# Perceiver on one core: the second layer's self attention with weights divided ahead of their turn, and scores and values in another matmul form

## The chip, the cores and the metric

The kernel runs on one core of a Trainium2 chip. The time is the device time of one execution in microseconds (us). TensorE multiplies matrices into PSUM, VectorE and ScalarE work element by element and read PSUM, GpSimd works on SBUF; they run at the same time and wait for each other by semaphores. A matmul has a stationary operand, loaded first, and a moving one that streams through. All work in the changed stage is fp32.

## The reference

x has 128 batches of 32 tokens with 128 features, the context 128 batches of 257 rows. Four layers follow each other, each a cross attention, a self attention and a feed-forward part, twelve stages in all, each added to x after a layer norm. The stage that is changed is the second layer's self attention (8 heads of 32, keys and values through a latent of 64):

```python
q = (x @ Wq.T).reshape(b, t, N_HEADS, HEAD_DIM)
kv_latent = x @ Wkv_down.T
k = (kv_latent @ Wk_up.T).reshape(b, t, N_HEADS, HEAD_DIM)
v = (kv_latent @ Wv_up.T).reshape(b, t, N_HEADS, HEAD_DIM)
scores = jnp.einsum('bqhd,bkhd->bhqk', q, k) * scale
attn = jax.nn.softmax(scores, axis=-1)
out = jnp.einsum('bhqk,bkhd->bqhd', attn, v)
out = out.reshape(b, t, N_HEADS * HEAD_DIM)
return out @ Wo.T
...
x = x + _L1_attn_ref(_layernorm(x, axis=-1), L1_attn_Wq, L1_attn_Wkv_down, L1_attn_Wk_up, L1_attn_Wv_up, L1_attn_Wo)
```

## The kernel before

x stays in SBUF as 32 tiles of 128 tokens, four batches of 32 each (NB = 4). The twelve stages run one after the other; at the end of each all five engines drain and wait for each other. `self_attention` writes the self attentions of the last three layers; `kind` tells them apart, and the changed stage is `"L1"` (layers are numbered from 0). Each engine has a function `one(r)` that issues its part of round r, and `Plan.run` calls it for the rounds from -3 to 32, the middle ones as a hardware loop of two rounds. The order in a round is the order of the lines, the same for all rounds. Rounds overlap: in round r the tile r + 3 gets its statistics, r + 2 is normalised, turned and projected, r + 1 gets its keys, values and scores, r its softmax, and r - 1 has its weights applied and is put out.

For one tile, the queries (256 features: 8 heads of 32) come as two halves n = 0, 1 of four heads, features on partitions. `rows_by_head` spreads each half into `qbd`: for each batch b a block of 128 columns, one for each pair of head j and query, that is zero outside the head's 32 features. In `scores` (L1039) such a block is the stationary operand, and the keys of its own batch, 32 columns, are the moving one. So the scores of one head and query lie on one partition, with 8 groups (half and batch) of 32 keys along it.

VectorE takes the maximum of each group (L1285) and subtracts it (L1287), ScalarE takes the exponential in place (L1209), and TensorE turns the undivided weights, 128 columns at a time (`turn`, L1062); ScalarE copies them to SBUF (L1132). Meanwhile VectorE sums the weights (L1300), takes reciprocals (L1301), and multiplies these with a mask of heads into `w` (L1302).

GpSimd writes `vm` (L933): the values of a tile once for each batch, zero outside that batch's rows. `values` (L1072) has the turned weights of a half as the stationary operand and 512 columns of `vm`, four batches by 128 features, as the moving one. The rows of the result are pairs of head and query; in each only the features of its own head are wanted. VectorE multiplies by `w`, which divides and clears the rest (L1268), and `heads` (L1084) sums the rows over the heads with eight matmuls by a window of a 0/1 matrix. The result is features by tokens; ScalarE copies it (L1167), `output` multiplies by Wo (L1092), and VectorE adds it to x (L1277).

On TensorE a round reads, in this order: `middle` (keys and values of the next tile from the latent, L1014, L1016), `values`, `turn_x` (L990), `turn` (L1062), `project` (L996, L998), `heads`, `scores`, `output`.

Of the kernel before, what the change touches and what calls it, by code (L numbers as in the profile page):

```python
# [881 lines left out]
def self_attention(k, kind, s):  # L882
# [9 lines left out]

    def chain_steps(has):
        if kind == "L1":
            return (["max"] * has.own + ["stats"] * has.third + ["rs", "rr", "w"] * has.own)
        if kind == "L2":
            return (["cos", "sin", "low", "high"] * has.coming + ["stats"] * has.third + ["rr", "w"] * has.turned
                    + ["ms"] * has.after)
        return (["E"] * has.own + ["rr", "w"] * has.turned + ["R", "max"] * has.own + ["stats"] * has.third)
# [9 lines left out]
    turned_written, turned_read, pv_done, heads_ready, heads_written, heads_read, out_written, out_read = (  # L909
        PerTile(k.sig(n), 1) for n in ("probs_T_written", "probs_T_read", "pv_done", "heads_ready", "heads_written",  # L910
                                       "heads_read", "out_written", "out_read"))
# [74 lines left out]
    def pe(pe):  # L986
# [44 lines left out]
        def scores(t):  # L1031
            pe.wait_ge(operands.sem, operands.at(t, 1))
            pe.wait_ge(scores_read.sem, scores_read.at(t + -1, 1))
            if kind == "L1":
                pe.wait_ge(mid_read.sem, mid_read.at(t, 1))
                for n in range(2):
                    for b in range(NB):
                        at = n * P + 32 * b
                        mm = pe.matmul(D[:, at:at + 32], s["qbd"][:, n, b * P:(b + 1) * P], s["kv"][:, at:at + 32],  # L1039
                                       start=True, stop=True, skip_group_check=True)  # L1040
            else:
                pe.wait_ge(spread.sem, spread.at(t, 1))
# [13 lines left out]
            mm.then_inc(scores_written.sem, 1)  # L1056
# [8 lines left out]
        def values(t):  # L1065
            pe.wait_ge(turned_read.sem, turned_read.at(t, 1))
            pe.wait_ge(vm_ready.sem, vm_ready.at(t, 1))
            pe.wait_ge(heads_ready.sem, heads_ready.at(t + -1, 1))
            for n in range(nt):
                left, vm = s["pT"][:, n * P:(n + 1) * P], s["vm"][:, t.odd, :]  # L1070
                if kind == "L1":
                    mm = pe.matmul(O[n][:, :], left, vm[:, n * 512:(n + 1) * 512], start=True, stop=True)  # L1072
                else:
                    pe.matmul(batches_first(O[0])[:, :, n, :], left, batches_first(vm)[:, :, n, :], start=True, stop=True,
                              skip_group_check=True)
                    mm = pe.matmul(SUM[:, 4 * n:4 * n + 4], left, k.c("quad"), start=True, stop=True, skip_group_check=True)
            mm.then_inc(pv_done.sem, 1)

        def heads(t):
            pe.wait_ge(heads_ready.sem, heads_ready.at(t, 1))  # L1080
            pe.wait_ge(out_read.sem, out_read.at(t + -1, 1))
            for n in range(2 if kind == "L1" else 1):
                for b in range(NB):
                    mm = pe.matmul(OUT[:, n * P:(n + 1) * P], s["om"][:, n, b * P:(b + 1) * P], window(k, b),  # L1084
                                   start=(b == 0 and n == 0), stop=(b == NB - 1), skip_group_check=True)
            mm.then_inc(heads_written.sem, 1)

        def output(t):
            pe.wait_ge(heads_read.sem, heads_read.at(t, 1))
            if kind == "L1":  # L1090
                for n in range(2):
                    mm = pe.matmul(OUT[:, 256:384], s["outT"][:, n, :], wo[:, n, :], start=(n == 0), stop=(n == 1),  # L1092
                                   skip_group_check=True)
            else:
                mm = pe.matmul(OUT[:, 256:384], s["outT"][:, 0, :], wo[:, :], start=True, stop=True, skip_group_check=True)
            mm.then_inc(out_written.sem, 1)

        def one(r):
# [3 lines left out]
                values(r.t + -1)  # L1102
            if r.after:
                turn_x(r.t + 2)
            if kind == "L1" and r.own:
                turn(r.t)
            if r.after:
                project(r.t + 2)
            if kind == "L2" and r.coming:
                middle(r.t + 1)  # L1110
            if kind == "L3" and r.coming:
                scores(r.t + 1)
            if r.turned:
                heads(r.t + -1)
            if kind == "L2" and r.own:
                turn(r.t)
            if kind != "L3" and r.coming:
                scores(r.t + 1)
            if kind == "L3" and r.own:
                turn(r.t)  # L1120
            if r.turned:
                output(r.t + -1)
# [5 lines left out]
    def act(act):  # L1128
# [33 lines left out]
                act.activation(s["qkT"], MID[:, 0:2 * P], ACT.Copy).then_inc(mid_read.sem, 1)  # L1162

        def take_heads(t):
            n = 2 if kind == "L1" else 1
            act.wait_ge(heads_written.sem, heads_written.at(t, 1))
            act.activation(s["outT"][:, 0:n, :], OUT[:, 0:n * P].rearrange("p (t c) -> p t c", t=n), ACT.Copy  # L1167
                           ).then_inc(heads_read.sem, 1)

        def one(r):  # L1170
            if kind != "L3" and r.turned:
# [32 lines left out]
            if kind == "L1":  # L1204
                if r.coming:
                    take_middle(r.t + 1)
                if r.own:
                    act.wait_ge(scores_read.sem, scores_read.at(r.t, 1))
                    act.activation(s["pr"][:, 0:256], s["pr"][:, 0:256], ACT.Exp).then_inc(probs_ready.sem, 1)  # L1209
# [19 lines left out]
    def dve(dve):  # L1229
# [27 lines left out]
        def heads(r):  # L1257
            if not r.turned:
                return
            t = r.t + -1  # L1260
            if kind != "L1":
                over_sums(r)
            dve.wait_ge(pv_done.sem, pv_done.at(t, 1))
            dve.wait_ge(heads_written.sem, heads_written.at(t + -1, 1))
            w = s["w"].rearrange("p u j -> p (u j)")
            for n in range(2 if kind == "L1" else 1):
                m = 16 if kind == "L1" else 64
                ins = dve.tensor_tensor(s["om"][:, n, :].rearrange("p (g d) -> p g d", d=hd),  # L1268
                                        O[n].rearrange("p (g d) -> p g d", d=hd), bc(w[:, n * m:(n + 1) * m], 2, hd), ALU.mult)
            ins.then_inc(heads_ready.sem, 1)  # L1270

        def residual(r):
            if r.ended if kind == "L2" else r.turned:
# [3 lines left out]
                dve.tensor_tensor(x, x, OUT[:, 256:384], ALU.add).then_inc(out_read.sem, 1)  # L1277

        def one_l1(r):
            sc, pr = D[:, 0:256].rearrange("p (u k) -> p u k", k=32), s["pr"][:, 0:256]  # L1280
            nm, w = s["nm"][:, 0:8], s["w"][:, 0:8, :]
            normalised(r)
            if r.own:
                dve.wait_ge(scores_written.sem, scores_written.at(r.t, 1))
                link(dve.tensor_reduce(nm, sc, X_AXIS, ALU.max, negate=True), r, "max")  # L1285
                dve.wait_ge(turned_written.sem, turned_written.at(r.t + -1, 1))
                dve.tensor_tensor(pr.rearrange("p (u k) -> p u k", k=32), sc, bc(nm, 2, 32), ALU.add  # L1287
                                  ).then_inc(scores_read.sem, 1)
            heads(r)
            if r.coming:  # L1290
                t = r.t + 1
                dve.wait_ge(qkv_read.sem, qkv_read.at(t, 1))
# [3 lines left out]
                ins.then_inc(operands.sem, 1)  # L1296
            stats(r)
            if r.own:
                dve.wait_ge(probs_ready.sem, probs_ready.at(r.t, 1))
                link(dve.tensor_reduce(s["rs"][:, 0:8], pr.rearrange("p (u k) -> p u k", k=32), X_AXIS, ALU.add), r, "rs")  # L1300
                link(dve.reciprocal(s["rr"][:, 0:8], s["rs"][:, 0:8]), r, "rr")  # L1301
                link(dve.tensor_tensor(w, bc(s["rr"][:, 0:8], 2, 4), bc(k.c("quad"), 1, 8), ALU.mult), r, "w")  # L1302
            residual(r)

        def rotate(r):
# [2542 lines left out]
```

## Time and profile before

| | |
|---|---|
| median of 3 runs | 5292.81 us (5286.52 to 6909.59) |
| profiled execution | 5294.46 us |
| its span | 5292.7 us |
| TensorE busy | 4721.4 us, 89% |
| VectorE busy | 3207.9 us, 61% |
| ScalarE busy | 2119.9 us, 40% |
| GpSimd busy | 1841.9 us, 35% |

The 6909.59 us are one execution of the three; the other two are 0.1% apart. The profile is of one execution. PE is TensorE's matmuls, PEld its weight loads, DVE VectorE, ACT ScalarE, POOL GpSimd. An fp32 matmul stands in the trace as two records, so counts of TensorE's rows are twice the matmuls in the code. PEclk is the clock that TensorE was granted, 1.00 being 2.4 GHz and 0.50 1.2 GHz. "Idle before" is the time that an engine sat idle before an instruction, with what released it.

### The profile page before, as it was taken

The numbers are of one execution on the slowest core, as the hardware profiler recorded it, in microseconds if no ns is written. First come the engines' busy times: TensorE is split into PE (matmuls) and PEld (weight loads), VectorE is DVE, ScalarE is ACT, GpSimd is POOL, SyncE is SP. The second block draws the span as 40 slices with busy tenths as digits, with TensorE's granted clock in tenths as the row PEclk, the third lists the DMA queues.
The fourth block names the chain that finished last, engine by engine and source line by source line (L and its number), as shares of the span: only waits on it lengthen the run. The fifth ranks groups of instructions, "written<-read, shape, count | busy, mean of one in ns | idle before, by whom it ended". The sixth has DMA issues, their size and how long they took to land.

```text
span 5292.7 us, 138451 instructions
## 1 busy us (share of the span) xinstructions
PE 4721.4 (89%) x48761; PEld 3730.1 (70%) x48761; DVE 3207.9 (61%) x9513; ACT 2119.9 (40%) x5243; POOL 1841.9 (35%) x2796
## 2 busy tenths in 40 slices
PE   4999999999999999896929999777999989997999
PEld 3777777779867777674627777665577768885776
DVE  4777777756546666565425666685466657764443
ACT  1444444422224444221214555342255545542333
POOL 2555555511113333334143433890034434430000
PEclk8999999999989999896968999898899998888999
DMA  6000000000000000000220100002211100005665
GB/s 201 18 18 18 18 18 18 18 1 2 1 21 29 32 28 25 0 0 20 70 63 29 36 32 28 1 0 55 58 33 32 32 21 0 0 0 114 144 143 134
DMA packets 112436, 199.69 MB, mean 38 GB/s; under 512 B 13315, under 2 KB 54659, under 8 KB 111259
## 3 DMA queue, kind: packets, MB, share of 16 engines
q1 hardware_dynamic: 108147, 188.67, 13.4%
q0 software_dynamic: 4096, 8.40, 0.6%
q8 instruction: 127, 2.08, 0.2%
q14 instruction: 66, 0.54, 0.0%
HBM read 183.29 MB, written 18.97 MB: 38 GB/s over the span
## 4 chain that ended last, share of the span: by engine, by line
PE 75%; DVE 7%; issue 6%; ACT 5%; POOL 4%; SPq 1%; DMA 1%; POOLq 1%; DVEq 0%; ACTq 0%
PE psum_banks L555 6%; PE psum_banks L3075 6%; PE psum_banks L3084 5%; PE psum_banks L560 5%; PE psum_banks L620 4%; PE psum_banks L664 4%; PE psum_banks L671 3%; PE psum_banks L1623 3%; PE psum_banks L624 3%; PE psum_banks L1658 2%; PE psum_banks L2103 2%; PE psum_banks L1084 2%; PE psum_banks L2770 2%; PE psum_banks L1599 2%; ACT scratch L1741 1%
## 5 line engine op out<-in xcount | busy, mean ns | idle before, releaser
L787 DVE TENSOR_REDUCE scratch<-psum_banks 128x2 f32<-128x514 f32 x768 | 531.6, 692 | 411.8 <-PE psum_banks L555 407.8
L706 ACT ACTIVATE scratch<-psum_banks 128x512 f32<-128x512 f32 x768 | 459.4, 598 | 490.0 <-PE psum_banks L565 474.4
L560 PE MATMUL psum_banks<-scratch 32*128 32x128 f32 x6144 | 639.6, 310 | 8.2 <-ACT scratch L706 6.1
L555 PE MATMUL psum_banks<-scratch 32*128 32x257 f32 x3072 | 575.2, 441 | 50.3 <-DVE scratch L788 50.0
L560 PEld LDWEIGHTS psum_banks<-scratch 32*128 32x128 f32 x6144 | 476.6, 185 | 17.5 <-ACT scratch L706 8.6
L555 PEld LDWEIGHTS psum_banks<-scratch 32*128 32x128 f32 x3072 | 253.9, 189 | 272.7 <-issue 175.9
L3084 PEld LDWEIGHTS psum_banks<-w_L_ffn_down,scratch 128*128 128x128 f32 (+1 forms) x2560 | 335.8, 193 | 156.0 <-issue 127.1
L3075 PE MATMUL psum_banks<-scratch,w_L_ffn_up 128*128 128x512 f32 (+1 forms) x752 | 382.0, 603 | 8.2 <-DVE scratch L3262 8.2
L3262 DVE TENSOR_TENSOR scratch<-scratch 128x512 f32<-128x512 f32 x304 | 210.3, 692 | 268.5 <-ACT scratch L3128 234.3
L3128 ACT ACTIVATE scratch<-psum_banks 128x512 f32<-128x512 f32 x320 | 191.0, 598 | 430.1 <-PE psum_banks L3075 430.0
L565 PE MATMUL psum_banks<-shift_T,own_batch 32*128 32x128 bf16 x3072 | 351.2, 215 | 0.0
L3084 PE MATMUL psum_banks<-w_L_ffn_down,scratch 128*128 128x128 f32 (+1 forms) x2560 | 342.7, 277 | 9.0 <-DVE scratch L3262 9.0
L620 PE MATMUL psum_banks<-scratch 128*32 128x128 f32 x6144 | 318.4, 279 | 1.5 <-ACT scratch L706 1.5
L624 PE MATMUL psum_banks<-scratch,consts 128*32 128x128 f32 x6144 | 309.2, 273 | 0.0
L1741 ACT ACTIVATE scratch<-psum_banks,scratch 128x258 f32<-128x258 f32 x512 | 238.6, 473 | 98.4 <-DVE scratch L1826 97.6
L728 ACT ACTIVATE scratch<-psum_banks,c_L_xattn_bk 128x256 f32<-128x256 f32 x384 | 182.8, 476 | 221.4 <-PE psum_banks L671 221.1
L1520 POOL TENSOR_TENSOR scratch<-scratch 128x512 f32<-128x512 f32 x256 | 269.3, 1052 | 0.0
L1599 PE MATMUL psum_banks<-scratch 128*128 128x257 f32 x1024 | 266.9, 383 | 1.3 <-ACT scratch L1758 0.8
L513 POOL TENSOR_TENSOR ln_vareps<-ln_meanvar,ln_eps 128x1 f32<-128x1 f32 x96 | 18.4, 191 | 716.1 <-DVE ln_meanvar L797 716.1
L1623 PE MATMUL psum_banks<-scratch 128*128 128x512 f32 x512 | 247.1, 604 | 11.4 <-ACT scratch L1751 10.6
L1599 PEld LDWEIGHTS psum_banks<-scratch 128*128 128x128 f32 x1024 | 179.7, 190 | 55.4 <-issue 39.8
L933 POOL TENSOR_TENSOR scratch<-scratch,consts 128x512 f32<-128x512 f32 x128 | 134.8, 1064 | 229.1 <-PE psum_banks L1072 139.6
(495 smaller groups left out, 12386.3 us busy)
## 6 DMA issues: line engine op xcount, KB each, us to landing
scratch<-route_T SPq DMA_DIRECT2D x136, 512.0 KB, 7.3
scratch<-in_ctx SPq DMA_DIRECT2D x99, 514.0 KB, 3.5
scratch<-in_ctx_rows SPq DMA_DIRECT2D x130, 128.0 KB, 2.0
scratch<-route_T SPq DMA_DIRECT2D x8, 1024.0 KB, 8.8
expert_rows<-in_ctx SPq DMA_DIRECT2D x10, 512.0 KB, 17.9
scratch<-expert_rows SPq DMA_DIRECT2D x16, 192.0 KB, 2.7
expert_out<-scratch SPq DMA_DIRECT2D x16, 192.0 KB, 2.1
w_L_ffn_up<-in_L_ffn_up SPq DMA_DIRECT2D x1, 2992.0 KB
```

The lines of the kernel that those rows point to most:

```text
L555: return pe.matmul(S[:, g % 2, :], qbd[q, t.odd, (s // 2) * P:(s // 2 + 1) * P], kT_of[q, t.odd, s // 2, :], start=True, stop=True)
L560: return pe.matmul(W[:, g % 2, c * P:(c + 1) * P], kT_of[q, t.odd, b, c * P:(c + 1) * P], qbd[q, t.odd, b * P:(b + 1) * P], start=True, st ...
L565: return pe.matmul(W[:, g % 2, c * P:(c + 1) * P], own_batch[q, b:b + 1].to_broadcast([32, P]), shiftT[q, t.odd, :], start=False, stop=Tru ...
L620: pe.matmul(PV[q, cols], vS[:, t.odd, b, c, q], pT[:, b % 2, g, c, :], start=False, stop=(c == 1), skip_group_check=True)
L624: mm = pe.matmul(SUM[q, cols], k.c("ones")[:, 0:32], pT[:, b % 2, g, c, :], start=False, stop=(c == 1), skip_group_check=True)
L706: act.activation(pT[:, b % 2, 2 * h:2 * h + 2].rearrange("p t c q -> p t (c q)"), W, ACT.Exp).then_inc(exp_ready.sem, 1)
L787: dve.tensor_reduce(parts[:, r.t.odd, 2 * h:2 * h + 2, 0, b], S, X_AXIS, ALU.max, negate=True)
L1599: mm = pe.matmul(S[:, t, 0:KEYS], qa[:, t, b * P:(b + 1) * P], a["zT"][:, b % 2, :], start=True, stop=True, skip_group_check=True)
L1623: mm = pe.matmul(PV[:, :], zk_of[:, b, c, :], a["pT"][:, c, :], start=(c == 0), stop=(c == 1))
L1741: ins = act.activation(a["p"][:, 4 * (b % 2) + t, :], S[:, t, 0:W], ACT.Exp, bias=a["negm"][:, u:u + 1], accum_out=a["rs"][:, u:u + 1])
L3075: mm = pe.matmul(U(u, o)[0:rows(c), :], up_cols(c, o), x, start=True, stop=True)
L3084: mm = pe.matmul(Y[g % 2][:, i * P:(i + 1) * P], a["h"][0:rows(c), u % 3, i * P:(i + 1) * P], down[0:rows(c), c, :], start=(c == 0 and i = ...
```

## The change

All of it is in the stage `"L1"` of `self_attention`:

- VectorE divides the weights by their sums itself (one product of 128x256), and the turn waits for that; the semaphore that ScalarE's exponential gives is now `exp_ready`, and `probs_ready` comes from VectorE. The small product into `w` and the two 128x512 products out of PSUM are gone.
- A block of queries is scored on the keys of all four batches: 128 moving columns for 32, into two PSUM banks instead of one. VectorE reads only the 32 keys of the block's own batch, in two instructions (one a bank) for the maximum and two for the subtraction.
- The values are now the stationary operand, in strips of 32 features (one head), and the turned weights, of all four heads of a group, are the moving one: 32 matmuls of 32x128 for 2 of 128x512. Each strip j writes partitions 32j to 32j + 31, so that the result has features on partitions.
- The sums over heads are gone; ScalarE copies, in four instructions of 32 partitions, for each head the columns that are its own.
- On TensorE the turn of the weights stands behind the scores.

```diff
-            return (["max"] * has.own + ["stats"] * has.third + ["rs", "rr", "w"] * has.own)
+            return (["max"] * has.own + ["stats"] * has.third + ["rs", "rr"] * has.own)
...
                 for n in range(2):
                     for b in range(NB):
-                        at = n * P + 32 * b
-                        mm = pe.matmul(D[:, at:at + 32], s["qbd"][:, n, b * P:(b + 1) * P], s["kv"][:, at:at + 32],
-                                       start=True, stop=True, skip_group_check=True)
+                        mm = pe.matmul(k.bank[n][:, b * P:(b + 1) * P], s["qbd"][:, n, b * P:(b + 1) * P],
+                                       s["kv"][:, n * P:(n + 1) * P], start=True, stop=True, skip_group_check=True)
...
-            pe.wait_ge(heads_ready.sem, heads_ready.at(t + -1, 1))
+            if kind == "L1":
+                pe.wait_ge(heads_read.sem, heads_read.at(t + -1, 1))
+            else:
+                pe.wait_ge(heads_ready.sem, heads_ready.at(t + -1, 1))
...
-                    mm = pe.matmul(O[n][:, :], left, vm[:, n * 512:(n + 1) * 512], start=True, stop=True)
+                    for b in range(NB):
+                        for j in range(4):
+                            d = slice(32 * j, 32 * j + 32)
+                            mm = pe.matmul(O[n][d, b * P:(b + 1) * P], vm[:, n * 512 + b * P + 32 * j:n * 512 + b * P + 32 * j + 32],
+                                           left, start=True, stop=True, skip_group_check=True)
...
-            if kind == "L1" and r.own:
-                turn(r.t)
             if r.after:
                 project(r.t + 2)
...
-            if r.turned:
+            if kind != "L1" and r.turned:
                 heads(r.t + -1)
...
-            if kind == "L3" and r.own:
+            if kind != "L2" and r.own:
                 turn(r.t)
...
+            if kind == "L1":
+                act.wait_ge(pv_done.sem, pv_done.at(t, 1))
+                act.wait_ge(out_written.sem, out_written.at(t + -1, 1))
+                for j in range(4):
+                    d = slice(32 * j, 32 * j + 32)
+                    ins = act.activation(s["outT"][d].rearrange("p n (b q) -> p n b q", q=32),
+                                         k.psum[d, 3:5, :].rearrange("p n (b c) -> p n b c", c=P)[:, :, :, d], ACT.Copy)
+                ins.then_inc(heads_read.sem, 1)
...
-                link(dve.tensor_reduce(nm, sc, X_AXIS, ALU.max, negate=True), r, "max")
+                for n in range(2):
+                    ins = dve.tensor_reduce(nm[:, 4 * n:4 * n + 4], own[n], X_AXIS, ALU.max, negate=True)
+                link(ins, r, "max")
...
-            heads(r)
...
-                link(dve.tensor_tensor(w, bc(s["rr"][:, 0:8], 2, 4), bc(k.c("quad"), 1, 8), ALU.mult), r, "w")
+                dve.tensor_tensor(by_head, by_head, bc(s["rr"][:, 0:8], 2, 32), ALU.mult).then_inc(probs_ready.sem, 1)
```

TensorE's instructions in the second round of the loop, before (the names in brackets are the semaphores waited for):

```order
L1072 MATMUL psum_banks<-scratch 128x512 [waits heads_ready,vm_ready,probs_T_read]
L1072 MATMUL psum_banks<-scratch 128x512
L988 REGISTER_ALU
L990 MATMUL psum_banks<-consts,x_normed 128x128 [waits qkv_read,xn_ready]
L1059 REGISTER_ALU
L1062 MATMUL psum_banks<-consts,scratch 128x128 [waits probs_T_read,probs_ready]
L1062 MATMUL psum_banks<-consts,scratch 128x128
L993 REGISTER_ALU
L996 MATMUL psum_banks<-x_normed_T,w_L_attn_Wq 128x128 [waits xT_read]
...
L1084 MATMUL psum_banks<-consts,scratch 128x128 x7
L1039 MATMUL psum_banks<-scratch 128x32 [waits mid_read,scores_read,operands_ready]
L1039 MATMUL psum_banks<-scratch 128x32 x7
L1092 MATMUL psum_banks<-w_L_attn_Wo,scratch 128x128 [waits heads_read]
```

and now (L1080 values, L993 turn of x, L999 and L1001 projections, L1041 scores, L1064 turn of the weights, L1101 output):

```order
L1080 MATMUL psum_banks<-scratch 32x128 [waits heads_read,vm_ready,probs_T_read]
L1080 MATMUL psum_banks<-scratch 32x128 x31
L991 REGISTER_ALU
L993 MATMUL psum_banks<-consts,x_normed 128x128 [waits qkv_read,xn_ready]
L996 REGISTER_ALU
L999 MATMUL psum_banks<-x_normed_T,w_L_attn_Wq 128x128 [waits xT_read]
...
L1041 MATMUL psum_banks<-scratch 128x128 [waits mid_read,scores_read,operands_ready]
L1041 MATMUL psum_banks<-scratch 128x128 x7
L1061 REGISTER_ALU
L1064 MATMUL psum_banks<-consts,scratch 128x128 [waits probs_T_read,probs_ready]
L1064 MATMUL psum_banks<-consts,scratch 128x128
L1101 MATMUL psum_banks<-w_L_attn_Wo,scratch 128x128 [waits out_read,heads_read]
```

The turn of the weights has moved from between the turn of x and the projections to behind the scores, the sums over heads are gone, and the values are 32 matmuls.

VectorE in a round, now, from the scores' arrival to the divided weights (L1296 maximum, L1300 subtraction, L931 spread queries, L1314 to L1316 sum, reciprocal, division):

```order
L1296 TENSOR_REDUCE scratch<-psum_banks 128x4 [waits scores_written]
L1296 TENSOR_REDUCE scratch<-psum_banks 128x4
L1246 REGISTER_ALU
L1300 TENSOR_TENSOR scratch<-psum_banks,scratch 128x128 [waits probs_T_written,vector_step]
L1300 TENSOR_TENSOR scratch<-psum_banks,scratch 128x128
L1305 REGISTER_ALU
L931 TENSOR_TENSOR scratch<-scratch,consts 128x512 [waits scores_written,qkv_read]
L931 TENSOR_TENSOR scratch<-scratch,consts 128x512
...
L1314 TENSOR_REDUCE scratch<-scratch 128x8 [waits exp_ready]
L1246 REGISTER_ALU
L1315 RECIPROCAL scratch<-scratch 128x8 [waits vector_step]
L1246 REGISTER_ALU
L1316 TENSOR_TENSOR scratch<-scratch 128x256 [waits vector_step]
```

Before, the two products with `w` stood between the subtraction and the spread queries; nothing stands there now.

## Rows read from the trace of the kernel before

**Rows 1.** The page: busy time, share of the span and instructions of each engine.
```profile
PE 4721.4 (89%) x48761; PEld 3730.1 (70%) x48761; DVE 3207.9 (61%) x9513; ACT 2119.9 (40%) x5243; POOL 1841.9 (35%) x2796
```

**Rows 2.** The stage: its us, PE, PEld, DVE, ACT, POOL busy, PEclk, DMA share, GB/s.
```profile
2126.50:2432.70 306.20, 292.63 (x1760) 221.23 (x1760) 180.28 (x448) 74.14 (x224) 88.93 (x128) 0.94 0.00 0
```

**Rows 3.** The chain of waits through one tile: start us, us, what.
```profile
2249.91 0.53 PE psum_banks L1092 x4
2250.44 0.64 PE psum_banks L1014 x4
2251.08 0.43 PE psum_banks L1016 x2
2251.51 1.91 PE psum_banks L1072 x4
2253.43 0.12 PE psum_banks L990
...
2253.57 0.29 ACT x_normed_T L1136
...
2253.90 0.71 PE psum_banks L996 x4
2254.61 0.36 PE psum_banks L998 x2
2254.98 1.98 PE psum_banks L1084 x16
2256.96 1.77 PE psum_banks L1039 x16
```

**Rows 4.** The timeline of the same tile: start us, us, engine, instruction, [idle before].
```profile
2250.60 0.29 DVE L1277 TENSOR_TENSOR x_tokens<-x_tokens,psum_banks 128x128 f32 x1 [1.49 <-PE psum_banks L1092]
...
2251.07 0.42 DVE L1285 TENSOR_REDUCE scratch<-psum_banks 128x8 f32<-128x256 f32 x1
...
2251.68 0.60 ACT L1160 ACTIVATE scratch<-psum_banks 128x512 f32<-128x512 f32 x1 [2.63 <-PE psum_banks L1016]
...
2253.26 0.27 PE L990 MATMUL psum_banks<-consts,x_normed 128*128 128x128 f32 x1
...
2253.37 0.38 PE L1062 MATMUL psum_banks<-consts,scratch 128*128 128x128 f32 x2
2253.46 1.29 DVE L1268 TENSOR_TENSOR scratch<-psum_banks,scratch 128x512 f32<-128x512 f32 x2 [1.52 <-PE psum_banks L1072]
...
2254.67 2.03 DVE L928 TENSOR_TENSOR scratch<-scratch,consts 128x512 f32<-128x512 f32 x2
...
2256.78 0.39 ACT L1143 ACTIVATE scratch<-psum_banks 128x256 f32<-128x256 f32 x1 [2.93 <-DVE scratch L928]
...
2257.06 0.26 ACT L1144 ACTIVATE scratch<-psum_banks 64x128 f32<-64x128 f32 x1
```

**Rows 5.** The chain in the cross attention: matmuls by column groups, 8 records a row.
```profile
1749.85 0.40 PE psum_banks L620 x8
1750.25 0.22 PE psum_banks L624 x8
```

**Rows 6.** TensorE's timeline, first and last outputs; the chain in a slow value stretch.
```profile
2159.94 0.47 PE L1092 MATMUL psum_banks<-w_L_attn_Wo,scratch 128*128 128x128 f32 x2
...
2410.06 0.69 PE L1092 MATMUL psum_banks<-w_L_attn_Wo,scratch 128*128 128x128 f32 x4
...
2431.58 0.60 PE L1092 MATMUL psum_banks<-w_L_attn_Wo,scratch 128*128 128x128 f32 x3 [0.47 <-ACT scratch L1167]
...
2205.76 3.61 PE psum_banks L1072 x4
```

**Rows 7.** TensorE early in the changed stage: us, PE busy, PEclk, DMA.
```profile
2145.00:2150.00 5.00, 5.00 (x22) 0.50 0.01 3
```

**Rows 8.** The fourth layer's self attention (as rows 2), the cross attention (as rows 7).
```profile
4360.00:4760.00 400.00, 369.57 (x2431) 336.96 (x2430) 283.73 (x562) 201.98 (x380) 156.11 (x186) 0.84 0.00 0
...
1745.00:1750.00 5.00, 3.83 (x76) 1.00 0.00 0
```

More of the change, by code:

```diff
@@ L908, in self_attention @@
     spread = PerTile(k.sig("operands_spread"), 1) if kind != "L1" else None
-    turned_written, turned_read, pv_done, heads_ready, heads_written, heads_read, out_written, out_read = (
-        PerTile(k.sig(n), 1) for n in ("probs_T_written", "probs_T_read", "pv_done", "heads_ready", "heads_written",
-                                       "heads_read", "out_written", "out_read"))
+    turned_written, turned_read, pv_done, heads_read, out_written, out_read = (
+        PerTile(k.sig(n), 1) for n in ("probs_T_written", "probs_T_read", "pv_done", "heads_read", "out_written", "out_read"))
+    if kind == "L1":
+        exp_ready = PerTile(k.sig("exp_ready"), 1)
+    else:
+        heads_ready, heads_written = PerTile(k.sig("heads_ready"), 1), PerTile(k.sig("heads_written"), 1)
     if kind == "L1":
@@ L1067, in values @@
             pe.wait_ge(vm_ready.sem, vm_ready.at(t, 1))
-            pe.wait_ge(heads_ready.sem, heads_ready.at(t + -1, 1))
+            if kind == "L1":
+                pe.wait_ge(heads_read.sem, heads_read.at(t + -1, 1))
+            else:
+                pe.wait_ge(heads_ready.sem, heads_ready.at(t + -1, 1))
             for n in range(nt):
@@ L1081, in heads @@
             pe.wait_ge(out_read.sem, out_read.at(t + -1, 1))
[L1082 to L1085, printed above, removed]
+            for b in range(NB):
+                mm = pe.matmul(OUT[:, 0:P], s["om"][:, 0, b * P:(b + 1) * P], window(k, b), start=(b == 0), stop=(b == NB - 1),
+                               skip_group_check=True)
             mm.then_inc(heads_written.sem, 1)
@@ L1090, in output @@
             if kind == "L1":
+                pe.wait_ge(out_read.sem, out_read.at(t + -1, 1))
                 for n in range(2):
@@ L1164, in take_heads @@
         def take_heads(t):
[L1165 to L1168, printed above, removed]
+            if kind == "L1":
+                act.wait_ge(pv_done.sem, pv_done.at(t, 1))
[5 more added lines that the diff above has]
+                ins.then_inc(heads_read.sem, 1)
+            else:
+                act.wait_ge(heads_written.sem, heads_written.at(t, 1))
+                act.activation(s["outT"][:, 0, :], OUT[:, 0:P], ACT.Copy).then_inc(heads_read.sem, 1)
         def one(r):
@@ L1208, in one @@
                     act.wait_ge(scores_read.sem, scores_read.at(r.t, 1))
-                    act.activation(s["pr"][:, 0:256], s["pr"][:, 0:256], ACT.Exp).then_inc(probs_ready.sem, 1)
+                    act.activation(s["pr"][:, 0:256], s["pr"][:, 0:256], ACT.Exp).then_inc(exp_ready.sem, 1)
             if kind == "L2" and r.own:
@@ L1260, in heads @@
             t = r.t + -1
-            if kind != "L1":
-                over_sums(r)
-            dve.wait_ge(pv_done.sem, pv_done.at(t, 1))
+            over_sums(r)
             dve.wait_ge(heads_written.sem, heads_written.at(t + -1, 1))
             w = s["w"].rearrange("p u j -> p (u j)")
[L1266 to L1270, printed above, removed]
+            dve.tensor_tensor(s["om"][:, 0, :].rearrange("p (g d) -> p g d", d=hd), O[0].rearrange("p (g d) -> p g d", d=hd),
+                              bc(w, 2, hd), ALU.mult).then_inc(heads_ready.sem, 1)
         def residual(r):
@@ L1279, in one_l1 @@
         def one_l1(r):
-            sc, pr = D[:, 0:256].rearrange("p (u k) -> p u k", k=32), s["pr"][:, 0:256]
-            nm, w = s["nm"][:, 0:8], s["w"][:, 0:8, :]
+            own = [k.bank[n].rearrange("p (m c) -> p m c", c=32)[:, 0:16:5, :] for n in range(2)]
+            pr = s["pr"][:, 0:256]
+            nm = s["nm"][:, 0:8]
             normalised(r)
@@ L1284, in one_l1 @@
                 dve.wait_ge(scores_written.sem, scores_written.at(r.t, 1))
-                link(dve.tensor_reduce(nm, sc, X_AXIS, ALU.max, negate=True), r, "max")
+                for n in range(2):
+                    ins = dve.tensor_reduce(nm[:, 4 * n:4 * n + 4], own[n], X_AXIS, ALU.max, negate=True)
+                link(ins, r, "max")
                 dve.wait_ge(turned_written.sem, turned_written.at(r.t + -1, 1))
-                dve.tensor_tensor(pr.rearrange("p (u k) -> p u k", k=32), sc, bc(nm, 2, 32), ALU.add
-                                  ).then_inc(scores_read.sem, 1)
-            heads(r)
+                for n in range(2):
+                    ins = dve.tensor_tensor(pr[:, n * P:(n + 1) * P].rearrange("p (u k) -> p u k", k=32), own[n],
+                                            bc(nm[:, 4 * n:4 * n + 4], 2, 32), ALU.add)
+                ins.then_inc(scores_read.sem, 1)
             if r.coming:
@@ L1298, in one_l1 @@
             if r.own:
-                dve.wait_ge(probs_ready.sem, probs_ready.at(r.t, 1))
-                link(dve.tensor_reduce(s["rs"][:, 0:8], pr.rearrange("p (u k) -> p u k", k=32), X_AXIS, ALU.add), r, "rs")
+                dve.wait_ge(exp_ready.sem, exp_ready.at(r.t, 1))
+                by_head = pr.rearrange("p (u k) -> p u k", k=32)
+                link(dve.tensor_reduce(s["rs"][:, 0:8], by_head, X_AXIS, ALU.add), r, "rs")
                 link(dve.reciprocal(s["rr"][:, 0:8], s["rs"][:, 0:8]), r, "rr")
-                link(dve.tensor_tensor(w, bc(s["rr"][:, 0:8], 2, 4), bc(k.c("quad"), 1, 8), ALU.mult), r, "w")
+                dve.tensor_tensor(by_head, by_head, bc(s["rr"][:, 0:8], 2, 32), ALU.mult).then_inc(probs_ready.sem, 1)
             residual(r)
```

## The prediction

> **What bounds the kernel now.** I read the page first: TensorE is busy for 89% of the span, the next engine, VectorE, for 61%, so what TensorE does in the changed stage is the first thing to look at [rows 1]. Twelve stages follow each other with a barrier between them, and only the fifth, the second layer's self attention, is touched; it lasts from 2126.5 to 2432.7 us, 306 us or 5.8% of the span, with TensorE busy for 292.6 us of it and hardly any DMA [rows 2]. Even a third off this stage would be 2% of the whole.
>
> Then the chain of waits for one tile in the middle of the stage [rows 3]. It runs on TensorE from piece to piece; the one place where TensorE waits is the copy of the turned x on ScalarE, 0.29 us and the small steps around it. Summed in order: output projection 0.53, keys and values from the latent 0.64 + 0.43, values applied to weights 1.91, turn of x 0.12, copy 0.35 with its steps, projections 0.71 + 0.36, block rows summed into heads 1.98, scores 1.77. That is 8.80 us a tile. The timeline of the same tile shows the other engines waiting for TensorE: VectorE idles 1.49 us before the residual, ScalarE 2.93 us before the copy of the queries [rows 4]. So a TensorE piece that goes away is gained in full, until another engine's path gets longer than what is left.
>
> **Part by part, for one tile at full clock.** Every fp32 matmul leaves two records in the trace, so the 8 sums over heads are 16 records.
>
> *Sums into heads, removed:* 16 records, -1.98 us [rows 3].
>
> *Scores on the keys of all batches:* still 16 records with a 128x128 stationary, but 128 moving columns in place of 32. The sums into heads have just this shape: 1.98 us against 1.77, so +0.21 us [rows 3]. A wider moving side is nearly free, since the weight load had been the limit.
>
> *Values applied to weights:* 4 records of 128x512 (1.91 us) become 64 records with a 128x32 stationary and 128 moving columns, which go to the four column groups in turn. The cross attention does the same: 8 such records take 0.40 us where the form begins and 0.22 us after that, 27 ns each [rows 5]. So 0.40 + 7 x 0.22 = 1.94 us, +0.03. The step 0.40 - 0.22 = 0.18 us is paid once a tile. The Trainium skill ("TensorEngine Tiling (Array Packing)", Key Properties) says that a change of tiling mode drains the engine; by that rule the return to the full array costs a second such step, 0.18 us more a tile and about 5 us in all, and the sum would be about 5245. No row isolates the way back.
>
> *The turn of the weights, moved:* before it stood between the turn of x and the projections, where TensorE waited for ScalarE's copy anyway, and cost nothing. Now it stands behind the scores with no wait to hide in, as the first order excerpt shows. Its two records show 0.38 us, with a tail that the next piece overlaps; the transpose ahead of it began 0.11 us earlier, so one may cost as little as 0.11 [rows 4]. Bounds 0.22 and 0.38; I take 0.25, nearer to the pitch than to the tail. The wait it leaves keeps its length.
>
> *VectorE:* the two 128x512 products out of PSUM go, 1.29 us [rows 4]. The small product becomes one of 128x256, which I price like the 128x256 reduction at 0.42; maximum and subtraction become two halves each, priced at 0.29 like the 128x128 residual, +0.16 a pair. Less work than before, and off the path: after the scores come output 0.53, a step of 0.17, residual 0.29, normalisation the same, maxima and differences 0.58 + 0.10 + 0.58, and the spread queries at worst 2.03 [rows 4]. The operands are ready 4.6 us after the scores' end. TensorE asks for them after 0.53 + 1.07 + 1.94 + 0.12 + 0.35 + 1.07 = 5.1 us. The divided weights need 0.5 for statistics and about 1.1 for sum, reciprocal and product more, 6.3 us; TensorE gets to the turn at 5.1 + 1.98 = 7.1. So the new wait, the turn for the product on VectorE, has 0.8 us of slack; if the slack went, the turn would hold the output and the next tile behind it.
>
> *ScalarE:* one 128x256 copy becomes four of 32 partitions x 256. Back to back, copies of 256 columns begin 0.28 us apart [rows 4]. From the end of the projections ScalarE does the queries' and latent's copies (0.44) and the four, 0.44 + 4 x 0.28 = 1.6 us with steps of 0.2; the output projection asks for them 1.98 + 0.25 = 2.2 us after the projections. A copy may cost 0.40 before TensorE waits. No row has 32 partitions: I take 0.28 from the nearest; below, nothing is gained, and above, the 128x512 copy's 0.60 bounds it (that is rival B). GpSimd has the same work and it becomes due no earlier in its round than before.
>
> Sum: 8.80 - 1.98 + 0.21 + 0.03 + 0.25 = 7.31 us a tile, **1.49 us less**.
>
> Over the stage: between the outputs at 2159.94 and 2410.06 us lie 250.1 us [rows 6], which are 28 rounds and two stretches in which the granted clock fell. 28 x 1.49 = 41.7 us. In each of the two stretches, at 2205.8 and 2260.3, the value matmuls took 3.6 us in place of 1.91 (the first is shown) [rows 6]; both follow on scores of 32 columns, a form that is gone, so 2 x 1.7 = 3.4 us. The clock stood at 1.2 GHz at the start until the first value matmuls had run, through two rounds of these scores, fully busy [rows 7]. With wider ones it may rise earlier: at least nothing, at most some 6 us (half of the 12 us of TensorE work there); I take 3. At the end, the last output begins 21.5 us after the one at 2410.06 [rows 6], in rounds that wait on a chain through all engines. Of that chain the product on VectorE (1.29) and the sums (1.98) go in each of the last rounds, and ScalarE's three more copies (0.84) and the wider product (0.23) come: about 2.2 less, three times, so 7 us. Sum 41.7 + 3.4 + 3 + 7 = 55 us. The profiled execution took 5294.46 us, its span 5292.7; the median of the runs shown, 5292.81, is the same within 0.03%. **Forecast 5240 us.** The instruction streams show that all of this is really in the program.
>
> **Rivals.**
>
> *A. The clock sinks.* The fourth layer's self attention is the warning: TensorE is busy there for 92% of 400 us, in pieces of 128 columns, and the mean granted clock is 0.84 [rows 8]. Against it: the cross attention, with the same column-group form as the new values, holds 1.00 while it runs [rows 5, 8]. At 0.84 a round takes 7.31 / 0.84 = 8.7 us, 28 x 0.1 = 3 us are left and half of the tail: 5288 us. At 1.2 GHz all through, a round would take twice 6.96 and the copy, 14.3 us, and the kernel about 5440. Chance 0.13 for the first, 0.02 for the second.
>
> *B. The four copies are dear.* At 0.60 us each they pass what scores and turn hide by 0.8 us a tile; 28 x 0.69 + 10 = 29 us remain: 5265. For it: PSUM is read in strips of 32 over two banks, which no row shows. Against it: all copies here cost by the number of columns. Chance 0.07.
>
> *C. The column groups do not run side by side*, **slower**. The place is the value matmuls. If each of the 64 records took what a full one takes in the sums, 1.98 / 16 = 0.124 us [rows 3], they would last 7.9 us, and a round 13.3: 28 x 4.5 + 11 at the ends = +137, 5430 us. From 53 ns a record on nothing is gained, from about 107 ns it is over 2% slower. For it: here all four groups get the same moving operand and only their stationaries differ, and no row has that. The Trainium skill ("TensorE: Matmul & The Clock Gate", Part 3, What overlaps and what doesn't) says that a weight load overlaps running matmuls only where the row group differs; here it never differs, and by that rule this is what would come. The trace disagrees: 27 ns a record with one row group. Chance 0.03.
>
> **How the numbers follow.** Forecast 0.74, A 0.15, B 0.07, C 0.03, 0.01 for something unforeseen and faster. The forecast's own bounds: the values at 27 ns throughout, the scores no dearer than before, the turn at 0.22 and the clock's whole 6 us make 16 us more gain (5.6, 5.9, 0.8 and 3); the turn at 0.38, a second mode step, nothing at either end and no gain at the start make about 20 us less: 5224 to 5260. The range reaches over B and into the first case of A, 5224 to 5286, and leaves out most of A, C and the odd case. 2% is 106 us, about what a measurement of this kernel tells surely from no change; the stage would have to lose a third. So faster by over 2% 0.01, slower 0.05 (C and the second case of A), the rest 0.94.
>
> **What would show it.** Right: outputs 7.2 to 7.5 us apart; chain still on TensorE with the ScalarE copy as the only stop; the 64 value records in 1.8 to 2.1 us; scores at about 2.0; idle before the output and before the turn near zero; granted clock 1.00 in every stretch after the first rounds; the stage about 250 us. Wrong: TensorE waiting for ScalarE ahead of the output (B), value records over 50 ns apart (C), the clock below 1.00 while TensorE is busy (A), or the turn waiting for VectorE's product.

## The result, and the profile after

The changed kernel takes 5234.06 us in the median of 4 runs (5223.27 to 5235.41), the kernel before 5293.6 us in the median of 4, one of them the 6909.59 us shown above, which is in a slower state and stays out of every ratio: the ratio is 0.9885, 95% interval 0.9868 to 0.9902. That is 1.15% faster, clear of the noise though under 2%, inside the range of the forecast (5224 to 5286) and 6 us from its 5240. The profiled execution took 5233.18 us.

The page and the stage, to be read beside [rows 1, 2]: only the changed stage differs in its instructions, and it is 56.5 us shorter (its first statistics to the next stage's: 2126.53 to 2432.97 before, 2126.20 to 2376.09 now).

```profile
PE 4657.2 (89%) x50169; PEld 3698.7 (71%) x50169; DVE 3165.2 (61%) x9513; ACT 2156.9 (41%) x5339; POOL 1845.0 (35%) x2796
```
```profile
2126.20:2376.00 249.80, 231.03 (x3168) 190.26 (x3168) 142.11 (x449) 113.48 (x320) 95.02 (x128) 0.97 0.00 0
```

The chain of waits through one round, to be read beside [rows 3] (L1017 and L1019 keys and values, L1080 values on weights, L993 turn of x, L999 and L1001 projections, L1041 scores, L1064 turn of the weights, L1101 output):

```profile
2249.97 0.64 PE psum_banks L1017 x4
2250.61 0.43 PE psum_banks L1019 x2
2251.04 1.88 PE psum_banks L1080 x64
2252.93 0.27 PE psum_banks L993
2253.20 0.02 issue
2253.22 0.29 ACT x_normed_T L1143
2253.51 0.04 issue
2253.55 0.71 PE psum_banks L999 x4
2254.26 0.36 PE psum_banks L1001 x2
2254.63 1.98 PE psum_banks L1041 x16
2256.61 0.22 PE psum_banks L1064 x2
2256.83 0.56 PE psum_banks L1101 x4
```

The next round begins at 2257.39: 7.42 us in place of 8.81, and the copy of x is still the only stop. The timeline of that round shows VectorE's division (L1316) and ScalarE's four copies (L1177), beside [rows 4]:

```profile
2254.32 1.18 DVE L1316 TENSOR_TENSOR scratch<-scratch 128x256 f32<-128x256 f32 x1
...
2255.10 1.52 ACT L1177 ACTIVATE scratch<-psum_banks 32x256 f32<-32x256 f32 x4
...
2256.34 0.25 PEld L1064 LDWEIGHTS psum_banks<-consts,scratch 128*128 128x128 f32 x2
...
2256.68 0.71 PE L1101 MATMUL psum_banks<-w_L_attn_Wo,scratch 128*128 128x128 f32 x4
```

The division ends at 2255.50, 0.84 us before the turn wants it (in every other round, where the division is shorter, 1.97 us before); the copies end at 2256.62, 0.06 us before the output starts. The clock, beside [rows 7], was granted in full from 2143 to 2370 us:

```profile
2143.00:2370.00 227.00, 215.41 (x3053) 1.00 0.00 0
```

The stage by its outputs (first at 2152.82, the 29th at 2360.51) against the forecast's parts:

| part | before | after | gained | forecast |
|---|---|---|---|---|
| start to first output | 33.4 | 26.6 | 6.8 | 3 |
| 28 rounds | 250.1 | 207.7 | 42.4 | 41.7 + 3.4 |
| 29th output to the end | 22.9 | 15.6 | 7.3 | 7 |
| stage | 306.4 | 249.9 | 56.5 | 55 |

The other 4.9 us between the two spans lie in stages without a change and are less than runs of one kernel differ by (5286.52 to 5294.38 us before). So of the forecast's 6 us of error, 1.5 are the stage's.

### The profile page after: what moved, and what is told of

Same layout as the page of the kernel before. It is cut to its first block, busy times and chain, and to the rows that moved or that the text cites. A ratio compares the mean times of both kernels' runs of the same rounds, so it can differ in the third digit from the quotient of the medians.

```text
span 5231.3 us, 141331 instructions
## 1 busy us (share of the span) xinstructions
PE 4657.2 (89%) x50169; PEld 3698.7 (71%) x50169; DVE 3165.2 (61%) x9513; ACT 2156.9 (41%) x5339; POOL 1845.0 (35%) x2796
## 4 chain that ended last, share of the span: by engine, by line
PE 75%; DVE 7%; issue 6%; ACT 5%; POOL 4%; SPq 1%; DMA 1%; POOLq 1%; DVEq 0%; ACTq 0%
PE psum_banks L555 6%; PE psum_banks L3089 6%; PE psum_banks L3098 5%; PE psum_banks L560 5%; PE psum_banks L620 4%; PE psum_banks L664 4%; PE psum_banks L671 3%; PE psum_banks L1637 3%; PE psum_banks L624 3%; PE psum_banks L1672 2%; PE psum_banks L2117 2%; PE psum_banks L2784 2%; PE psum_banks L1613 2%; ACT scratch L1755 1%; PE psum_banks L2104 1%
```

## The experiments

Each starts from the changed kernel unless said otherwise. The kernel before, timed again beside each set of runs, took 5294 and 5310 us on one chip and 5314 us on another; so ratios are to it. Where a difference between two kernels is small, the stage in the two traces is compared as well: from its first statistics to the next stage's it takes 306.4 us before and 249.9 us in the changed kernel.

**Narrow scores.**

```diff
-                        mm = pe.matmul(k.bank[n][:, b * P:(b + 1) * P], s["qbd"][:, n, b * P:(b + 1) * P],
-                                       s["kv"][:, n * P:(n + 1) * P], ...
+                        own = slice(b * P + 32 * b, b * P + 32 * b + 32)
+                        keys = slice(n * P + 32 * b, n * P + 32 * b + 32)
+                        mm = pe.matmul(k.bank[n][:, own], s["qbd"][:, n, b * P:(b + 1) * P], s["kv"][:, keys], ...
```

> The changed kernel with one part undone: a block of queries is scored on the 32 keys of its own batch alone again (written to the same columns of the same two banks). Theory (the wide form costs 0.21 us a round, but takes away the stretches in which the clock was at 1.2 GHz): rounds of 7.2 us in place of 7.41, 28 x 0.21 = 6 us gained; the first output is about 6 us later in the stage than in the changed kernel (26.6 us after its start), because the clock rises only with the first value matmuls, and one or more stretches under 1.00 come back in the middle. Sum 5230 to 5238, no difference to the changed kernel's 5234. Rival (the clock does not follow the scores' form): first output still at 26 to 27 us, granted clock 1.00 from there on, 5228 us.

5260.47 us, ratio 0.9947 (0.9930 to 0.9963): 26 us slower than the changed kernel by the medians, 33 by the ratios. The stage takes 282.8 us, 32.9 more than in the changed kernel: 5.9 at the start, 24.4 in the 28 rounds, 2.6 at the end. A round at full clock, then TensorE in three stretches:

```profile
2254.73 1.90 PE psum_banks L1043 x16
2256.63 0.25 PE psum_banks L1066 x2
2256.88 0.61 PE psum_banks L1103 x4
```
```profile
2145.00:2150.00 5.00, 5.00 (x23) 0.50 0.00 0
2265.00:2270.00 5.00, 5.00 (x60) 0.50 0.00 0
2330.00:2335.00 5.00, 5.00 (x31) 0.72 0.00 0
```

Scores, turn and output sum to 2.76 us, just as with wide scores (1.98 + 0.22 + 0.56): a round at full clock is 7.42 us either way, and the score records start 0.112 us apart with 32 moving columns as with 128. But the clock falls to 1.2 GHz in stretches all through the stage, the mean round is 8.29 us, the mean clock of the stage 0.84, and the first output comes at 2159.01. The theory's mechanism was right, its size far off: narrow scores bring the falls back, and many more than the two that the kernel before had. What in the stream of instructions brings a fall about is not shown: TensorE was busy for 7.63 of the 8 us before the one at 2264.

**Wide scores alone**, in the kernel before (the scores and VectorE's halves as in the change, nothing else; VectorE's lines are left out here).

```diff
-                        mm = pe.matmul(D[:, at:at + 32], s["qbd"][:, n, b * P:(b + 1) * P], s["kv"][:, at:at + 32], ...
+                        mm = pe.matmul(k.bank[n][:, b * P:(b + 1) * P], s["qbd"][:, n, b * P:(b + 1) * P],
+                                       s["kv"][:, n * P:(n + 1) * P], ...
```

> The kernel before with one part of the change alone: a block of queries is scored on the keys of all four batches (128 moving columns), into two banks, and VectorE takes maximum and differences in two halves. Theory (after the run with narrow scores: wide scores cost nothing at full clock, and keep the clock up): rounds of 8.8 us as before, first output 26 to 27 us after the stage's start in place of 33.4, granted clock 1.00 from there on without the two falls; 6.8 + 3.4 = 10 us gained, 5283 us. Rival (they cost 0.21 us a round as the sums' rows say): 28 x 0.21 = 6 us less gain, 5289 us. Rival (the clock's falls have nothing to do with them): 5293 to 5299 us.

Ratio 0.9985 (0.9973 to 0.9997), 8 to 11 us. Rounds of 8.81 us, but for the last of the 28 at 8.87 as in the kernel before; first output at 2154.35, no fall. The stage takes 297.4 us, 9.0 less than before: 5.6 at the start, 3.4 in the rounds. In its chain the sums (L1083) and scores (L1038) are of one shape, 16 records each:

```profile
2256.41 2.04 PE psum_banks L1083 x16
2258.45 1.79 PE psum_banks L1038 x16
```

So 128 moving columns cost nothing over 32 that can be seen here (1.79 against 1.77 us). The 0.2 us go to whichever 16 records come first after the projections: the sums before, the scores now.

**The turn back in its old place** (`turn` between `turn_x` and `project`).

```diff
+            if kind == "L1" and r.own:
+                turn(r.t)
             if r.after:
                 project(r.t + 2)
...
-            if kind != "L2" and r.own:
+            if kind == "L3" and r.own:
                 turn(r.t)
```

> The changed kernel with the turn of the weights back between the turn of x and the projections. Theory (the divided weights are not there yet at that place): TensorE reaches the turn 3.2 us after an output's end, VectorE's product ends 4.4 to 5.5 us after it, so TensorE waits for VectorE, 1.2 to 2.3 us less the 0.35 us of ScalarE's copy of x that is hidden now: rounds of 8.3 to 9.4 us, 5260 to 5290 us. Rival (VectorE has slack enough to move its work forward): no wait, the turn's 0.22 us hidden, rounds of 7.2 us, 5228 us.

5285.61 us, ratio 0.9987 (0.9978 to 0.9997). TensorE waits for the division:

```profile
2259.21 0.44 PE L1064 MATMUL psum_banks<-consts,scratch 128*128 128x128 f32 x2 [1.23 <-DVE scratch L1318]
```

Rounds are 8.35 to 10.99 us, 9.26 in the mean, as expected in kind and partly longer, for the clock falls here too, though the scores are wide: of the 7.4 us before the fall at 2177.5 TensorE was busy for 5.0. So wide scores do not keep the clock up by themselves. In this kernel the division ahead of the turn pays only with the turn behind the scores; in the old place it eats nearly the whole gain.

**The value matmuls by one group, and by two groups, at a time.**

```diff
-                    for b in range(NB):
-                        for j in range(4):
+                    for j in range(4):
+                        for b in range(NB):
```

> The changed kernel with the value matmuls in another order: all four batches of one column group, then the next group, in place of the four groups in turn. The same 64 records. Theory (the 27 ns a record come from four column groups that work side by side, and take turns in the order of the program): neighbours in one group wait for each other, about 0.107 us a record as in a full matmul of 128 columns, 64 records in 6.9 us, rounds of 12.4 us, 5390 us. Rival (27 ns is the price of the weight load of 32 columns, whatever the order): no change, rounds of 7.41 us, 5234 us.

```diff
+                    for b, j in ((b, j) for i in (0, 2) for b in range(NB) for j in (i, i + 1)):
```

> The changed kernel with the value matmuls alternating between two column groups (first groups 0 and 1 for all batches, then 2 and 3) in place of four. Theory (a group by itself takes 67 ns a record, as the run with one group showed, and groups work side by side, until the weight loads set 27 ns): 67 / 2 = 33 ns a record, 64 records in 2.1 us, rounds of 7.65 us. Rival (all that counts is that neighbours are in different groups): 1.88 us, rounds of 7.41 us.

One group: 5304.45 us, ratio 1.0018 (1.0007 to 1.0029), rounds of 9.79 us. Two groups: 5271.25 us in one run, rounds of 7.95 us. The value matmuls in their chains, one group first:

```profile
2254.63 4.26 PE psum_banks L1080 x64
```
```profile
2251.19 2.42 PE psum_banks L1080 x64
```

In the mean 67 ns a record in one group, 38 in two in turn, 29 in four. The order alone makes 2.4 us a round (4.26 against 1.88), more than the 1.40 that the whole change gains, so the rival in which the order does not count is out. The other theory, 0.107 us a record, is right for neighbours and wrong for the sum, as the starts of the records show. The first four in one group at a time, and the first twelve in four groups, both from the timeline:

```profile
2254.56 0.62 PE L1080 MATMUL psum_banks<-scratch 128*32 128x128 f32 x4
...
2250.97 0.54 PE L1080 MATMUL psum_banks<-scratch 128*32 128x128 f32 x12
```

A single record is shown 0.27 us long. In one group at a time the records start 0.110 us apart (the second 0.133 after the first); 0.47 us after the first, a second series starts with the same pace and runs beside the rest of the first, and so on, eight series in all. With two groups in turn the records start in pairs, with series again 0.47 us apart, four of them. With four they start four at a time, 0.110 us apart, without series. The trace does not name the column group of a record, but eight records fit one group's series, and the sums come out: seven times 0.47 us, and about 1 us for the last series, are 4.3 us; three times 0.47 and about 1 us are 2.4. So a column group takes a record every 0.110 us, just as the full array does (0.112 in the scores), whatever the order, and the order says how many groups work side by side. Why the next series starts in the middle of one is not shown. The 33 ns expected for two groups were worked out from the mean of 67, which holds that overlap already.

One group at a time lengthens the stage to 325.6 us, two groups to 266.7 us.

**A fifth copy.**

```diff
+                act.activation(s["om"][0:32, 0, 0:256]..., k.psum[0:32, 3:5, :]..., ACT.Copy)
                 for j in range(4):
...
```

> The changed kernel with a fifth copy on ScalarE ahead of the four (the same 32 partitions x 256 out of PSUM, written where nobody reads). Theory (the four copies take 0.38 us each and end only 0.06 us before the output projection starts, so that their path and TensorE's are of one length): 0.3 us more a round, TensorE idle before the output, rounds of 7.7 us, 5243 us. Rival (there is slack on ScalarE that the profile does not show, since TensorE's queue reads ahead): rounds of 7.41 us, 5234 us.

Ratio 0.9907 (0.9880 to 0.9935), rounds of 7.68 us, and the chain goes over ScalarE:

```profile
2259.99 0.37 ACT scratch L1179
2260.38 0.39 ACT scratch L1179
2260.76 0.04 issue
2260.81 0.38 PE psum_banks L1101
```

0.27 us of the 0.38 show: the copies' path had 0.1 us of slack. The stage is 8.4 us longer.

**The turn of x between the halves of the values.**

```diff
-                values(r.t + -1)
+                values(r.t + -1, (0,) if kind == "L1" else None)
             if r.after:
                 turn_x(r.t + 2)
+            if kind == "L1" and r.turned:
+                values(r.t + -1, (1,))
```

> The changed kernel with the turn of x between the two halves of the value matmuls in place of behind them. Theory (each return from column groups to the full array costs a step of about 0.15 us and each entry 0.18 us; the changed kernel pays one pair a round, this one pays two, but the second half of the values hides ScalarE's copy of x, 0.35 us): rounds of 7.41 - 0.35 + 0.33 = 7.4 us, 5234 us, with 0.27 us for the turn of x, again about 0.27 for the first record of the projections, and no idle time for the copy of x. Rival (the step is not from the change of form): the turn of x at 0.12 us, rounds of 7.06 us, 5224 us.

Ratio 0.9852 (0.9825 to 0.9878), rounds of 7.12 us.

```profile
2253.18 1.01 PE psum_banks L1080 x32
2254.19 0.26 PE psum_banks L993
2254.45 1.01 PE psum_banks L1080 x32
2255.46 0.64 PE psum_banks L999 x4
```

The copy of x is hidden, and the stage takes 241.3 us, 8.6 less than in the changed kernel. The two halves of the values take 2.02 us in place of 1.88, 0.14 more; the turn of x 0.26; the projections 0.64 in place of 0.71. The theory priced the second pair at 0.33 and was wrong by more than half. It added a step for the return to projections that pay a start either way: 0.71 us after the wait, 0.64 behind the column groups, against 0.45 for four records at 0.112.

**Keys and values behind the turn of x**, and a version with the heads' copies moved too. ScalarE's order follows (its lines are left out here).

```diff
-            if kind != "L2" and r.coming:
+            if kind == "L3" and r.coming:
                 middle(r.t + 1)
...
                 turn_x(r.t + 2)
+            if kind == "L1" and r.coming:
+                middle(r.t + 1)
```

> The changed kernel with the matmuls for keys and values of the next tile (four and two records) moved from the round's beginning to between the turn of x and the projections, and ScalarE's order to match (copy of x, exponential, copy of keys and values, copy of queries). Theory (the one stop left on TensorE is the wait for the copy of x, 0.35 us, and any work put there hides it): rounds of 7.06 us, 28 x 0.35 = 10 us gained, 5224 us. Rival (ScalarE's four copies end only 0.06 us before the output wants them, so that any shift on ScalarE comes back as a wait before the output): rounds of 7.3 us or more with TensorE idle before the output, 5230 us or more.

> The changed kernel again, on the chip on which the next runs are timed. All theories: ratio to the kernel before 0.9885 as on record, rounds of 7.41 us.

> The kernel with the keys' and values' matmuls behind the turn of x again, beside the changed kernel on one chip. Theory (0.43 us a round less than the changed kernel, 1.5 us less at the start): 28 x 0.43 + 1.5 = 13.5 us less than it, ratio to the kernel before 0.986. Rival (its lower time in the first comparison was the chip's): no difference to the changed kernel, 0.9885.

5216.56 us, ratio 0.9855 (0.9838 to 0.9871). On one chip: the changed kernel 5244.35 us, 0.9880 (0.9863 to 0.9897), this one 5232.27 us, 0.9855 (0.9841 to 0.9870), 12 us apart; the intervals overlap a little, but the traces tell the two apart: rounds of 7.41 against 6.98 and 7.12 in turn, 7.05 in the mean, and the stage 249.6 against 238.1 us. That is 0.37 us a round, not the 0.43 expected.

```profile
2256.11 0.56 PE psum_banks L1101 x4
2256.66 0.07 issue
2256.74 1.96 PE psum_banks L1080 x64
2258.69 0.26 PE psum_banks L993
2258.95 0.64 PE psum_banks L1017 x4
```

Nothing on ScalarE stands in this chain, which is the theory; the 0.14 us of every second round stand at the values, 0.07 as a stop ahead of them and 0.08 in them, from a cause that this chain does not name.

```diff
+            if kind == "L1" and r.turned:
+                take_heads(r.t + -1)
             if r.after:
                 take_qkv(r.t + 2)
```

> The kernel with the keys' and values' matmuls moved behind the turn of x, and ScalarE's four copies of the heads moved ahead of its copies of queries and latent. Theory (TensorE alone sets the round now, 6.98 us): no further gain in time, 5217 us, but the copies end about 0.9 us before the output wants them. Rival (in the run without this move the copies held the output now and then, as the 0.07 us stops in its chain hint): rounds of 6.9 us, 5214 us.

> The kernel with the matmuls moved and the four copies of the heads ahead of the queries' copy, with a fifth copy on ScalarE. Theory (the order gives ScalarE 0.9 us of slack, so that the fifth copy's 0.38 us is hidden, while it cost the changed kernel 0.28 us a round): rounds of 6.97 us, no stop before the output. Rival (ScalarE's sum, 4.2 us and more, or its waits bind wherever the copies stand): rounds of 7.2 us or more.

With the heads' copies first: ratio 0.9863 (0.9837 to 0.9889), rounds of 7.04 us. With the fifth copy on top: 0.9866 (0.9840 to 0.9892), 7.04 us again. The copy that cost 0.27 us a round in the changed kernel costs nothing here, so this order has the slack; the forecast of 6.97 for every round was 0.07 too low in both. What binds there is another copy of ScalarE's: in the rounds of 7.12 us the chain goes over the copy of the turned weights (L1141), for which the values wait.

```profile
2258.41 0.04 issue
2258.45 0.39 ACT scratch L1141
2258.84 0.12 issue
2258.97 1.95 PE psum_banks L1080 x64
```

(From the run with five copies.) So with the keys and values moved, TensorE's chain and one over that copy are nearly of one length.

## Why the prediction was right

**The bound.** TensorE's chain set the stage before and after, and no other engine took over: that carried the forecast, and with it the sign. The trace and the fifth copy show how near the others are. ScalarE has 0.06 to 0.1 us: a copy of 32 partitions takes 0.38 us back to back, not 0.28, and the prediction had said that 0.40 would make TensorE wait, so this held by 0.02 us a copy, which is luck. VectorE has 0.84 us (forecast 0.8), but by two errors that cancel: the spread queries end earlier (1.28 us for the 2.03 taken at worst), and the division takes 1.18 us, not 0.42.

**The terms of a round** (forecast, measured): sums -1.98, -1.98; scores +0.21, +0.21; values +0.03, -0.03; turn of the weights +0.25, +0.22; output 0, +0.03; turn of x 0, +0.15. Together -1.49 against -1.40. The scores' term was right in size and wrong in cause: its 0.21 us go with the place behind the projections, as the narrow form in the changed kernel (1.90 us) and the wide form in the kernel before (1.79) show, not with the columns. The turn of x is the term that was left out. The rule that a change of tiling mode drains the engine (the Trainium skill, "TensorEngine Tiling (Array Packing)", Key Properties) was named in the prediction at 0.18 us and kept out of its sum. The rows agree with it: where the form of the stationary changes, a piece takes 0.12 to 0.19 us more than its records at 0.110 or 0.112 (scores after the 64 columns of the latent's projection 1.98 for 16, keys after the output 0.64 for 4, values after the 64 rows of the keys and values 1.88 for 16 fours), and the turn of x after the values 0.27 in place of 0.12; where it stays, the turn of the weights takes 0.22 for 2, nothing more. Only the output, 0.56 for 4 in an unchanged form, does not fit. That is a reading of the rows; no run changes the form alone.

**The clock** was the largest error in size. I gave it 3 + 3.4 us; the start of the stage gained 6.8 us, 5.6 of which the wide scores alone bring, and the falls 3.4. The error was made good by the rounds: 28 times 0.09 us, 2.5 us, less than forecast. So the sum of 55 for 56.5 is nearer than its terms, and that is luck. What was missed: with narrow scores the changed kernel would have met rival A's mechanism, at its mean clock of 0.84, with rounds of 8.29 us where rival A had 8.7, and lost 33 of the stage's 56.5 us. That the four steps are one change matters here.

**Rival C** lay nearer than its chance of 0.03 says for another order of the same loop: at one group at a time the kernel is 0.18% slower than before. As written, the groups alternate, and the row of the cross attention (27 ns) held within 3 ns (29). The rule cited there (the Trainium skill, "TensorE: Matmul & The Clock Gate", Part 3, What overlaps and what doesn't) would let no weight load overlap a running matmul in any order, since the row group never differs; the runs disagree with it, with four records in 0.110 us.

**The ends.** 7 us forecast, 7.3 measured, in the last three rounds as forecast: 3.2, 2.1 and 2.1 us.

## What to carry to other kernels

When work is cut out of a chain on one engine, price each piece that now follows another neighbour, not the removed ones alone: the first piece after a change of place or form carries the step. Where matmuls go to column groups, let the groups alternate in the innermost loop. Before a matmul is made narrower, look at what the granted clock does: here moving columns that nobody reads were free, and leaving them out cost 33 us in the stage.

## What the runs showed that was not expected

- In the changed kernel, narrow moving operands in the scores go with a granted clock that falls to 1.2 GHz while TensorE stays fully busy: 5.00 us busy in 5 us at 0.50, where the wide form has 1.00.
- VectorE's division of 128x256, SBUF to SBUF, takes 0.55 us in one round and 1.18 us in the next; I had priced it at 0.42. GpSimd is at work beside it in both, so what makes the difference is not shown.
- Four records of 32 stationary columns, one to each column group, start together every 0.110 us, where the full array starts one record every 0.112 us.
